# Where each node's edges begin in the two sorted lists: counted by one-hot rows, or found by a search of ranks

## What is computed

```python
e = leaky_relu(h_l[row] + h_r[col], ALPHA)                      # 100,000 edges, 4 heads of 64
m = segment_max(e, row); ex = exp(e - m[row])
out = segment_sum((ex / segment_sum(ex, row)[row])[:, :, None] * h[col], row)
...
e = leaky_relu(a_src[src] + a_dst[dst])                         # 131,072 edges in list 2
scores = layernorm(agg + b_gat).reshape(M, HEADS, NUM_EXPERTS).mean(1)   # top 2, softmax
out = sum over experts of g * (gelu(x @ W1 + b1) @ W2 + b2)
```

## Time and profile before

| | us |
|---|---|
| median of 3 runs | 4602.96 (4595.94 to 4609.97) |
| the profiled execution's own time | 4600.72 |
| its span | 4599.0 |
| PE busy, DVE busy, POOL busy | 1994.8, 1905.6, 1901.0 |
| chain that ended last: unknown queue, PE, DVE | 19%, 16%, 7% |

### The profile page before, as it was taken

One profiled execution on the slowest core, in us unless ns is written; L12 is line 12 of the kernel. 1 busy time (PEld: TensorE's weight loads), 2 busy tenths in 40 slices (PEclk: granted clock), 3 DMA queues, 4 the chain that ended last, 5 costly groups with the idle time before them and its releaser, 6 DMA issues. The chain is left out here.

```text
span 4599.0 us, 28729 instructions
## 1 busy us (share of the span) xinstructions
PE 1994.8 (43%) x8658; PEld 1511.8 (33%) x8658; DVE 1905.6 (41%) x3756; ACT 590.9 (13%) x1135; POOL 1901.0 (41%) x1909
## 2 busy tenths in 40 slices
PE   5236033444434453555541244435464443446720
PEld 3125022322223342434430133324343332334510
DVE  7789555444644643536510121121222112222657
ACT  4100011111111111111310001101010100101000
POOL 0015735445445544441767434444333344432032
PEclk9555566666666665656565667768787776778855
DMA  3111333443443433334521011111101011110415
GB/s 123 17 37 26 92 132 114 139 141 113 143 137 110 151 133 107 132 121 155 137 66 16 12 27 21 20 28 27 27 18 33 14 20 28 28 27 18 151 50 185
DMA packets 196305, 353.72 MB, mean 77 GB/s; under 512 B 55253, under 2 KB 160651, under 8 KB 192792
## 3 DMA queue, kind: packets, MB, share of 16 engines
q0 software_dynamic: 73264, 122.12, 12.2%
q1 hardware_dynamic: 73823, 181.16, 10.8%
q10 hardware_dynamic: 49132, 49.53, 3.2%
HBM read 181.17 MB, written 171.59 MB: 77 GB/s over the span
## 5 line engine op out<-in xcount | busy, mean ns | idle before, releaser
L533 POOL DMA_INDIRECT at_ring<-table,e_col x872 | 828.9, 951 | 1064.9 <-DMA at_sums<-at_ring 803.2
L1744 POOL DMA_INDIRECT at_ring<-table,at_idx x792 | 804.7, 1016 | 253.2 <-issue 233.9
L1808 PE MATMUL at_psS<-at_ring,at_hot 128*128 128x260 f32 x1584 | 578.6, 528 | 633.5 <-issue 371.5
L1808 PEld LDWEIGHTS at_psS<-at_ring,at_hot 128*128 128x128 f32 x1584 | 381.9, 260 | 825.0 <-issue 538.5
L769 PE MATMUL pick_rows<-pick_table,late_space 128*128 128x272 bf16 x1368 | 212.2, 314 | 703.6 <-issue 359.8
L1305 PE MATMUL ffn_psH<-xnT,late_space 128*128 x896 | 385.0, 591 | 196.6 <-ACT late_space L1340 188.5
L1368 DVE TENSOR_TENSOR late_space<-ffn_psY,ffn_b 128x256 f32<-128x256 f32 x196 | 82.5, 424 | 915.9 <-PE ffn_psY L1316 492.2
L1316 PE MATMUL ffn_psY<-late_space 128*128 128x256 f32 x1568 | 381.3, 405 | 162.6 <-issue 91.4
L769 PEld LDWEIGHTS pick_rows<-pick_table,late_space 128*128 128x128 bf16 x1368 | 143.5, 109 | 760.6 <-issue 364.7
L1316 PEld LDWEIGHTS ffn_psY<-late_space 128*128 128x128 f32 x1568 | 316.8, 204 | 224.8 <-issue 102.8
L1305 PEld LDWEIGHTS ffn_psH<-xnT,late_space 128*128 128x128 f32 x896 | 276.6, 312 | 297.4 <-ACT late_space L1340 196.3
(11 more groups left out here) (349 smaller groups left out, 2253.6 us busy)
## 6 DMA issues: line engine op xcount, KB each, us to landing
at_sums<-at_ring SPq DMA_DIRECT2D x24, 4356.0 KB, 12.1
products<-late_space ACTq DMA_DIRECT2D x28, 896.0 KB
late_space<-products SPq DMA_DIRECT2D x16, 896.0 KB, 11.7
at_ring<-table,e_col POOLq DMA_INDIRECT x872
at_ring<-table,at_idx POOLq DMA_INDIRECT x792
at_sums<-at_ring SPq DMA_DIRECT2D x16, 768.0 KB, 3.2
late_space<-products ACTq DMA_DIRECT2D x12, 896.0 KB, 11.2
table<-np_rows SPq DMA_DIRECT2D x7, 910.0 KB, 4.2
```

Source lines behind the costliest of these rows:

```text
L533: g.indirect_dma_start(self.ring[z][:, k, 0:TW], None, self.table, bass.IndirectOffsetOnAxis(ap=self.runs.col[:, u * U + k:u * U + k + 1], ...
L1744: g.indirect_dma_start(self.ring[z][:, k, 0:self.TW], None, self.table, bass.IndirectOffsetOnAxis(ap=self.idx[:, z, k:k + 1], axis=0)).the ...
L1808: last = pe.matmul(self.psS[at % 2][:, k - lo, 0:TW], self.hot[:, b, k, :], rows[:, b * self.SUB + k, 0:TW], start=True, stop=True)
```

## The change

`Counts` goes and `Ranks` comes. For each partition of the sorted list, `past` holds for each node a 0 or 1, whether the partition begins beyond the node; it is one comparison of 128 x 49 x 128 elements on VectorE. `differences` holds the codes of a partition less those of the partition ahead of it, in two parts exact in bf16. A matmul of a tile's `past` with the two parts (L375, L376) therefore brings, for each node on a lane, the codes of the one partition in which its first edge must lie. VectorE then counts along 400 or 512 elements how many are less than the node (L383, `is_lt` with a sum), twice a tile: 98 such operations and 196 matmuls for each list. 49 one-column matmuls over `past` count the whole partitions ahead, and two matmuls by `shift` and `corner` bring the next node's position, from which counts and last positions follow.

The codes of the partition ahead are loaded a second time. For list 1 SP loads them with the others; for list 2 ScalarE's queue copies them behind its last `take_sums` of the sorting units, and `Runs.read` waits for them (`s_prior`). List 2 has one tile ahead of the loop and 16 in each round. Apart from that, the exponentials of the second attention go to PSUM; the weights are copied once into the rows, and the scans over them run there in place.

```diff
@@ -290,117 +290,148 @@
-class CountTiles:
+class RankTiles:
...
+        self.past, self.parts = sb("past", [P, T, P], BF16), sb("parts", [P, 2, SLOTS], BF16)
...
+        self.ps = [tiles.psum[:, i * 512:i * 512 + J // 2] for i in range(2)]
+        self.ps_many, self.ps_next = tiles.psum[:, 0:tiles.T], tiles.psum[:, 512:512 + tiles.T]
...
+    def past(self, v, code):
+        q, t, T, c = self.q, self.t, self.t.T, self.c
+        tile = c["iota16"][:, 0:T]
+        q.step(v.memset(t.one[:, :], 1.0))
+        q.step(v.memset(t.first[:, T:T + 1], float(self.edges)))
+        q.step(v.tensor_scalar(t.lane[:, :], c["part_id"][:, :], float(1 << COL_BITS), None, ALU.mult))
+        q.step(v.tensor_scalar(t.row_i[:, :], code[:, 0:1], ((1 << ROW_BITS) - 1) << COL_BITS, None, ALU.bitwise_and))
+        q.wait()
+        q.step(v.tensor_scalar(t.node[:, :], tile, float(1 << (COL_BITS + LANE_BITS)), t.lane[:, 0:1], ALU.mult, ALU.add))
+        q.step(v.tensor_scalar(t.row[:, :], t.row_i[:, :], 1.0 / (1 << COL_BITS), None, ALU.mult))
+        q.wait()
+        q.step(v.tensor_scalar(t.first_row[:, :], tile, -float(P), t.row[:, 0:1], ALU.mult, ALU.add))
+        q.wait()
+        q.step(v.tensor_tensor(t.past[:, :, :], self.iota.unsqueeze(1).to_broadcast([P, T, P]),
+                               t.first_row[:, :].unsqueeze(2).to_broadcast([P, T, P]), ALU.is_gt))
...
+    def differences(self, v, code, prior, one, two):
+        bits = ROW_BITS - LANE_BITS
+        for part, mask in enumerate((((1 << bits) - 1) << (COL_BITS + LANE_BITS), (P - 1) << COL_BITS)):
+            q.step(v.tensor_scalar(one, code, mask, None, ALU.bitwise_and))
+            q.step(v.tensor_scalar(two, prior, mask, None, ALU.bitwise_and))
+            q.wait()
+            q.step(v.tensor_tensor(t.parts[:, part, 0:J], one, two, ALU.subtract))
+            q.wait()
+        v.sem_inc(self.s_parts, 1)
...
+    def begin_rows(self, pe):
+        pe.sem_inc(self.s_used, 2)
+        pe.wait_ge(self.s_parts, 1)
+    def rows(self, pe, at, first, i):
+        t, H = self.t, self.H
+        past = t.past[:, bass.ds(at + i, 1), :].rearrange("p o q -> p (o q)")
+        for half in range(2):
+            pe.wait_ge(self.s_used, first * 2 + (2 * i + half + 1))
+            pe.matmul(self.ps[half], past, t.parts[:, 0, half * H:(half + 1) * H], start=True, stop=False)
+            pe.matmul(self.ps[half], past, t.parts[:, 1, half * H:(half + 1) * H], start=False, stop=True)\
+                .then_inc(self.s_rows, 1)
+    def below(self, v, at, first, i):
+        t, H = self.t, self.H
+        for half in range(2):
+            v.wait_ge(self.s_rows, first * 2 + (2 * i + half + 1))
+            v.tensor_scalar(t.less[:, half, 0:H], self.ps[half], t.node[:, bass.ds(at + i, 1)], 0.0, ALU.is_lt, ALU.add,
+                            accum_out=t.n[:, bass.ds(at + i, 1), half]).then_inc(self.s_used, 1)
+    def end_rows(self, pe):
+        t, T = self.t, self.t.T
+        pe.wait_ge(self.s_used, 2 * T + 2)
+        for i in range(T):
+            last = pe.matmul(self.ps_many[:, i:i + 1], t.past[:, i, :], t.one[:, :], start=True, stop=True)
+        last.then_inc(self.s_many, 1)
+        pe.wait_ge(self.s_first, 1)
+        pe.matmul(self.ps_next, t.shift[:, :], t.first[:, 0:T], start=True, stop=False)
+        pe.matmul(self.ps_next, t.corner[:, :], t.first[:, 1:T + 1], start=False, stop=True).then_inc(self.s_next, 1)
+    def positions(self, v, start_idx):
...
+        v.wait_ge(self.s_used, 2 * T + 2)
+        do(v.tensor_tensor(t.many[:, :], t.n[:, :, 0], t.n[:, :, 1], ALU.add))
+        v.wait_ge(self.s_many, 1)
+        do(v.tensor_scalar(t.before_t[:, :], self.ps_many, 1.0, float(self.J), ALU.subtract, ALU.mult))
+        do(v.tensor_tensor(t.many[:, :], t.many[:, :], t.before_t[:, :], ALU.add))
+        do(v.tensor_scalar(t.first[:, 0:T], t.many[:, :], 0.0, None, ALU.max))
+        v.sem_inc(self.s_first, 1)
+        v.wait_ge(self.s_next, 1)
...
+    def load_prior(self, a):
+        a.wait_ge(self.s_sorted, self.sorted)
+        a.dma_start(self.prior[1:P, :].bitcast(F32), self.code[0:P - 1, :]).then_inc(self.s_prior, 16)
...
-        self.counts.lanes(v, code, self.itmp[:, :])
+        q.step(v.memset(self.prior[0:1, :], 0))
+        self.ranks.past(v, code)
+        q.step(v.tensor_scalar(x.col[:, :], code, (1 << COL_BITS) - 1, None, ALU.bitwise_and))
+        v.wait_ge(self.s_prior, 16)
+        q.wait()
+        self.ranks.differences(v, code, self.prior, self.itmp[:, :], self.same[:, :].bitcast(I32))
         do(v.tensor_scalar(self.itmp[:, :], code, COL_BITS, (1 << ROW_BITS) - 1,
                            ALU.logical_shift_right, ALU.bitwise_and))
-        q.step(v.tensor_copy(self.rowf, self.itmp[:, :]))
-        q.step(v.tensor_scalar(x.col[:, :], code, (1 << COL_BITS) - 1, None, ALU.bitwise_and))
-        q.wait()
+        do(v.tensor_copy(self.rowf, self.itmp[:, :]))
...
-        self.factor = sb("factor", [P, 2, HEADS, U])
+        self.factor = ctx.enter_context(nc.psum_tensor(f"{tag}_factor", [P, 2, HEADS, U], F32))
...
+        q.step(v.tensor_copy(rows[:, :, D:D + HEADS], weight.rearrange("p h u -> p u h")))
         q.wait()
         for h in range(HEADS):
-            q.step(v.tensor_tensor_scan(rows[:, :, D + h], decay[:, h, :], weight[:, h, :],
+            q.step(v.tensor_tensor_scan(rows[:, :, D + h], decay[:, h, :], rows[:, :, D + h],
                                         self.carry[:, D + h:D + h + 1], ALU.mult, ALU.add))
...
-        sp.dma_start(self.even, self.flat[0:P * self.J].bitcast(I32).rearrange("(p j) -> p j", p=P)).then_inc(self.s_even, 16)
+        codes = self.flat[0:P * self.J].bitcast(I32).rearrange("(p j) -> p j", p=P)
+        sp.dma_start(self.even, codes).then_inc(self.s_even, 16)
+        sp.dma_start(self.prior[1:P, :], codes[0:P - 1, :]).then_inc(self.s_even, 16)
         sp.dma_start(self.by_chain, self.flat[0:x.slots].rearrange("(p m) -> p m", p=CHAINS)).then_inc(self.s_chain, 16)
...
-        v.wait_ge(self.s_even, 16)
-        counts.lanes(v, self.even, self.itmp)
+        v.wait_ge(self.s_even, 32)
+        v.wait_ge(self.att.s_iota, 1)
+        ranks.past(v, self.even)
         v.wait_ge(self.s_turn, 1)
...
-        per_round = self.J // counts.GROUP // self.COUNT_ROUNDS
-        with v.Fori(0, self.COUNT_ROUNDS) as r:
-            for i in range(per_round):
-                counts.hots(v, r, per_round, i)
-        counts.positions(v, x.start_idx[:, :])
+        ranks.differences(v, self.even, self.prior, self.itmp, self.itmp2)
+        for t in range(x.T):
+            ranks.below(v, 0, 0, t)
+        ranks.positions(v, x.start_idx[:, :])
...
         pe.wait_ge(self.s_colf, 1)
         self.turn_index(pe, 0, self.colf.rearrange("p g (k l) -> p g k l", k=self.index.steps))
-        counts.begin_counts(pe)
-        per_round = self.J // counts.GROUP // self.COUNT_ROUNDS
-        with pe.Fori(0, self.COUNT_ROUNDS) as r:
-            for i in range(per_round):
-                counts.counts(pe, r, per_round, i)
-        counts.end_counts(pe)
+        ranks.begin_rows(pe)
+        for t in range(self.index.T):
+            ranks.rows(pe, 0, 0, t)
+        ranks.end_rows(pe)
...
             rest = chains.steps - SHORT_ROUNDS - TURNING
-            ahead, per_round = 8, 40
-            shares = [range(0, 7), range(7, 14), range(14, 20), range(20, 27), range(27, 33), range(33, per_round)]
-            assert 2 * TURNING == LONG and (ahead + per_round * rest) * Counts.GROUP == J2
+            ahead, per_round = 1, 16
+            shares = [range(0, 3), range(3, 6), range(6, 9), range(9, 11), range(11, 14), range(14, per_round)]
+            assert 2 * TURNING == LONG and ahead + per_round * rest == T
 @@ -2203,19 +2236,19 @@
                         order2.turn_back(pe, r * 2 + 1)
                         att.turn_scores(pe, n, 2)
                         att.add_runs(pe, n, 2)
-                    found2.counts.begin_counts(pe)
+                    found2.ranks.begin_rows(pe)
                     for i in range(ahead):
-                        found2.counts.counts(pe, 0, 0, i)
+                        found2.ranks.rows(pe, 0, 0, i)
                     with pe.Fori(0, rest) as r:
                         n = counter(r, SHORT_ROUNDS + TURNING)
                         for z in range(GROUPS):
                             att.turn_scores(pe, n, z)
                             for i in shares[2 * z]:
-                                found2.counts.counts(pe, r, per_round, ahead + i)
+                                found2.ranks.rows(pe, r * per_round + ahead, r * per_round + ahead, i)
                             att.add_runs(pe, n, z)
                             for i in shares[2 * z + 1]:
-                                found2.counts.counts(pe, r, per_round, ahead + i)
-                    found2.counts.end_counts(pe)
+                                found2.ranks.rows(pe, r * per_round + ahead, r * per_round + ahead, i)
```

(8 more changed lines are left out.)

120 lines of the change are left out of this document (42 added, 78 removed).

## The result

The change takes 4646.48 us (median of 4 runs, 4643.60 to 4654.88) and the kernel before, beside it, 4599.45 (4 runs, 4595.83 to 4609.97). The ratio is 1.0097, with a 95% interval of 1.0080 to 1.0115: about 45 us slower. The forecast was 4639. The profiled execution of the change has a span of 4653.0 us, 54.0 more than that of before, and a granted clock of 0.666 instead of 0.658.

A forecast was written before the change was run, and what follows sets the result against it. Counts on VectorE were the first index's path; in later units, matmul records left behind the gather by TensorE's spell delay stores. 4600.7 +10 +8 +16 +2 = 4636.7, with 2.2 for the median 4639; own range 4623 to 4657, overall 4567 to 4669.

The forecast's parts named there:

- First index, +10: List 1's index up to the first scatter: tiles meet the spell, scatter at 426, +10 us (+4 to +20).
- The spell: While GpSimd gathers at full pace, TensorE all but stops; in the first index from 342, at 2.5 us a matmul.
- `read`, +8: Second list's `read`: the wait for shifted codes delays L1853 by 12.6 us, pushing 22 to 26 records behind the gather, +8.
- I take 5.7: In `read` of the second list: the shifted copy of the sorted codes was taken to need 5.7 us, until 1563.
- The shares, +16: List 2's tiles in the first attention's later units: later records, wide tiles held by the spell, +16 us (-5 to +35).
- The records behind the gathers: A unit's matmul records left between gather's end and store, 0.33 us each: 66 in two units, 25 to 50 in others.
- Exponentials in PSUM, +2: Second attention, 16 units: new copy +4, scans 0, rows' rounding -1, in all +2 us (-8 to +11).
- (a): Rival: no spell in the first index, -14 in place of +10, total 4615; chance 0.16.
- (c): Rival: the spell charges by instruction, so fewer count matmuls leave fewer records behind gathers, -34, total 4569; chance 0.30.
- (b): Rival: the spell charges by column, so 512-column matmuls wait twice as long, +68, total 4671; chance 0.16.

The follow-up runs named there:

- A: Condition of a run set that no kernel chose: the kernel before takes 4600 to 4629 us; the forecast and the result stand under it.
- B: The other condition that no kernel chose: every kernel takes about two thirds of its time, before 3144 to 3149 us, and no trace shows the spell.
- list 1 by ranks: The change on the first list alone, its load in two pieces, exponentials in PSUM, list 2 counted as before: 4612.69 us, 1.0015 of before, under A.
- the slower gather: The change with both copies cut into 112 and 15 partitions and a 384-element GpSimd fill before each first-index gather: 4617.30 us, 0.9968 of before, under A.
- the narrow matmuls: The change with both copies cut and each 400-column matmul of list 1's tiles issued as two of 200: 4653.85 us, one execution, under A.

## Why the prediction was right, point by point

**Its direction and its size** were right (4639 forecast, 4646 measured), and the first term's mechanism was that foretold. But part of the agreement is luck: the copies made two terms too small by 29 us and the shares were too large by 12. By the first scatter and the unit of `read`, the change with both copies in two pieces would be some 21 us faster (11 and 10, above), an estimate, since that kernel has no run under A: about half the loss.

**First index, +10: measured +22.** The tiles came at 1.23 us (1.25), and a gather took 0.95 us. From the last tile to the scatter it took 4.9 us, the 49 one-column matmuls with 1.38 of them; the forecast had 10.4 (5 and 5.4), 5.5 too many. The spell came 12 us behind the last slowed gather, as in the earlier trace rows, and cost 28 to 30: 438.6 less 410.5 (one piece, A and B) and 427.3 less 397.5 (two pieces). I had 24, and the two errors, 5 in the spell and 5.5 behind the tiles, cancel: with two pieces the scatter is at 427.3 and the forecast was 426. It doesn't begin at once: the waits of VectorE for half a tile grow to 4.94 us; from 355 to 381 TensorE made 14 matmuls, 1.9 us each, less than my 2.5. What I had not counted is the end: from 382 to 400 the change makes 39 matmuls where 58 fit (list 1 by ranks, whose spell is over by then), 6 us. Most of it is the spell itself, which goes on for 5 us behind the last gather, to 386.74; the rest is the lower clock, which in the change is granted until 392 (0.70 is the mean of the 18 us). *The step that failed* is "I take it as covered; uncovered it costs at most 3 us" on the added load of the codes: 13 us. I had priced the transfer by its bytes, from a store of 4,356 KB that lands in 12.25 us. That store has 128 partitions and this load 127. The window's DMA share of 0.06 shows one engine at work, and the run with two pieces shows that the number of partitions was the reason. The Trainium skill has the rule, in DMA: Bandwidth & Descriptors, Why a DMA increments its semaphore by 16 and not by 1: the number of engines is the largest up to 16 that divides the slowest dimension of both sides. By that 127 partitions get one and 112 get sixteen. The trace agrees, and I had not weighed it.

**`read`, +8: measured +24.** The same step failed again, "I take 5.7": 40 us landed beside the store. In two pieces it takes 11, still double my figure. The sequence behind it was sized well (12.9 us from the wait's end to L1885, forecast 12.6). The delay's price was worked out as 22 to 26 records pushed behind the gather; all 66 were. With the copy at 40 us that is the delay alone: L1885 begins at 1633.01 and the gather ends at 1639.60, ahead of every tile of the unit's shares and every one of its records. With the copy at 11 us it is the share's tiles, which fall into the spell and hold the records back; the unit is then +15, just outside my 0 to +14.

**The shares, +16: measured +4** (-4.5 in the six units, +8.6 in the last two). The sum had a slip as well: half of what 28 records cost is 4.6 us by its own 0.33, and it took 8. The records behind the gathers were 40 to 44, inside the 25 to 50 forecast, but not 66 in two: the wide tiles make the units alike, and the two worst of before (58 and 46) improved. I had counted the delay on top of each unit of before. The rows fit another reading, that what decides is where the spell catches the unit, and that this place is now the same in all; no run tests it. In the last two units I had a tile at 1.38 us; rows show 1.71 us at a granted clock of 1.00 and 2.15 at 0.50. Only two halves of PSUM pass between the engines, and between the half tiles VectorE waits 0.28 us for L376 at the one clock and 0.57 at the other:

```profile
2107.72 0.75 DVE L383 TENSOR_SCALAR_CACHE_REDUCE rank_less<-turned,rank_node 128x512 bf16<-128x512 f32 x1
...
2109.43 0.75 DVE L383 TENSOR_SCALAR_CACHE_REDUCE rank_less<-turned,rank_node 128x512 bf16<-128x512 f32 x1
...
2126.16 0.75 DVE L383 TENSOR_SCALAR_CACHE_REDUCE rank_less<-turned,rank_node 128x512 bf16<-128x512 f32 x1
...
2128.31 0.75 DVE L383 TENSOR_SCALAR_CACHE_REDUCE rank_less<-turned,rank_node 128x512 bf16<-128x512 f32 x1
```

**Exponentials in PSUM, +2:** right under A.

**The rivals.** (a), no spell in the first index, is what B and the slower gather show: with the load in two pieces 397.5 and 397.8, where I had 402. The condition was rightly named for A, a gather at full pace; under B it isn't enough. (c), a charge by instruction with 4569, fell as a forecast: it needed under 1 us a matmul in the spell, and rows show 2.8 (half tiles of 5.6 us). But its mechanism is the one that the narrow matmuls bear out, and (b), by column, is the one that they don't. My 2.5 for 400 columns was near the price at full strength all the same. Why the charge goes by the matmul stays open. The pages of the profiles of the change and of the kernel with the factor in SBUF, with the spell and without it, list the same packets on the two queues for instructions (23 and 51, 0.0% of the time), so they give no sign of a wait for code.

**A part left unexplained.** The stage from store 0 to store 14 has the same program in all kernels and took 945.5 to 962.1 us under A: 958.4 to 962.1 in the three kernels of the set in which before took 4629.44, and 945.5 to 950.2 elsewhere. So times of different sets can't be set against each other. The kernel with the slower first gather takes 29 us less than the change; but against the before of its own set it is 12 us faster, where the change is 43 slower. That is 55 us, near the 51 by the marks (41 at the first scatter, 10 in `read`).

## What to carry to other kernels

Before pricing a copy by its bytes, look at its partitions: 127 in one piece used one DMA engine of sixteen and took 22 and 40 us, 112 and 15 in two pieces took under 9 and 11. When VectorE's two-operand work beside a gather goes away, ask what the gather does at full pace to the others; here it stopped TensorE, and a small fill between the gathers took that away for nothing, since the gather had slack. Where such a stall can't be avoided, few wide matmuls are cheaper in it than many narrow ones (2.8 us for 512 columns, 2.5 for 200). A delay ahead of a stall is not added to it: ask at which point of the unit the stall catches the work.

## What the runs showed of the hardware

- One and the same program took 4600 or 3149 us. Under B TensorE never stopped beside a gather of 0.95 us and 1.25 us pitch; 14 units took 593 instead of 950 us. What sets the condition stays open, and so does what the spell is: only that a pitch of 1.66 us instead of 1.25 is enough to be rid of it under A, where from 352 to 380 us the DMA engines move 81 instead of 106 GB/s (the change).
- A gather can be shut out altogether. In the second profile of before, in the first index, GpSimd's row between the hot rows reads:

```profile
350.57 61.26 POOL L1744 DMA_INDIRECT at_ring<-table,at_idx  x1 [0.30 <-issue]
412.14 0.95 POOL L1744 DMA_INDIRECT at_ring<-table,at_idx  x1 [0.31 <-issue]
```

One gather took 61.26 us, until VectorE's operations with two SBUF operands ended, and the first scatter came at 442.9 instead of 416.3. So the change's +22 in the first index holds against the first profile of before; against this one it would be -4. In how many executions of before it happens isn't known. The Trainium skill, SBUF — State Buffer, Who interferes with whom, calls the shared ports an exclusive lock between VectorE and GpSimd, held for a whole instruction, and infers that `tensor_tensor` leaves the making of descriptors alone. The row fits a lock, but neither the inference nor a wait of one instruction: it spans more than a hundred operations of VectorE. The change has two such operations left, beside the first two gathers of this index.
- From the end of a fill by GpSimd to the gather that waits for its end stand 0.27 us, and 0.79 with a semaphore increment between the wait and the gather, whether the wait compares with a constant or with a counted value.
- At the spell's full strength a matmul costs 2.5 to 2.8 us whether it has 200, 400 or 512 columns.
